# Attention kernel on one core: rotary sine terms by exchanging even and odd partitions in SBUF

## What is computed

```python
xn = _layernorm(x, ln1_g, ln1_b)
q = _l2norm((xn @ Wq).reshape(Bx, Tx, H, Dh))
k = _l2norm((xn @ Wk).reshape(Bx, Tx, H, Dh))
q = _rope(q, times)
k = _rope(k, times)
...
# _rope
xr = x.reshape(*x.shape[:-1], half, 2)
x1, x2 = (xr[..., 0], xr[..., 1])
r1 = x1 * cos - x2 * sin
r2 = x1 * sin + x2 * cos
```

## Time and profile before

| what | value |
|---|---|
| runs | 2165.68, 2159.67, 2165.37 us, median 2165.37 |
| profiled execution | span 2164.4 us; its own time is not given apart from the three above, the span is 1.0 us below their median |
| granted TensorE clock, mean | 0.931 of 2.4 GHz; 1.00 in the stretches of attention from 50 to 650 us |
| 300 to 350 us (attention), busy of 50 us | TensorE 48.06, VectorE 40.44, ScalarE 43.75, GpSimd 12.59 |
| a full step, from one start of L807 to the next | 41.83 us (324.63 to 366.46) |
| 300 to 350 us, DMA | 9% of the 16 engines, 28 GB/s |

### The profile page before, as it was taken

One profiled execution on the slowest core, in us unless ns is written; L12 is line 12 of the kernel. 1 busy time (PEld: TensorE's weight loads), 2 busy tenths in 40 slices (PEclk: granted clock), 3 DMA queues, 4 the chain that ended last, 5 costly groups with the idle time before them and its releaser, 6 DMA issues. The chain is left out here.

```text
span 2164.4 us, 37241 instructions
## 1 busy us (share of the span) xinstructions
PE 1849.2 (85%) x12576; PEld 954.5 (44%) x12600; DVE 1703.8 (79%) x3547; ACT 1474.7 (68%) x2917; POOL 1165.1 (54%) x720
## 2 busy tenths in 40 slices
PE   6999999999998459957889889898898988659996
PEld 2566666656665259952222222222222222124453
DVE  7778868877863437854899999999999998976776
ACT  5888888888885138845656666666666666437775
POOL 2122232242221027871789999999999998840001
PEclk9999999999999669977899999999999998879998
DMA  4100010011001012221100111001111100023333
GB/s 169 36 26 26 28 49 26 26 36 41 21 25 33 20 50 77 88 72 42 30 25 27 34 35 34 27 30 30 31 35 35 35 31 30 21 67 90 97 84 78
DMA packets 103708, 97.35 MB, mean 45 GB/s; under 512 B 9137, under 2 KB 86113, under 8 KB 103137
## 3 DMA queue, kind: packets, MB, share of 16 engines
q1 hardware_dynamic: 95584, 75.34, 12.4%
q0 software_dynamic: 6784, 18.10, 2.5%
q10 hardware_dynamic: 1152, 1.54, 0.2%
HBM read 45.87 MB, written 28.10 MB: 34 GB/s over the span
## 5 line engine op out<-in xcount | busy, mean ns | idle before, releaser
L1935 POOL TENSOR_TENSOR hc<-h,c_rep 128x1024 f32<-128x1024 f32 x256 | 627.8, 2463 | 137.9 <-DVE h L1899 136.7
L1899 DVE TENSOR_TENSOR_SCAN h<-decay,bank 128x1024 f32<-128x1024 f32 x241 | 551.0, 2286 | 22.5 <-issue 0.9
L1757 ACT ACTIVATE decay<-bank,neg_a_r 128x510 f32<-128x510 f32 x512 | 322.6, 683 | 257.5 <-PE bank L1634 257.1
L1618 PE MATMUL bank<-u_in,sel_rows 32*128 32x512 f32 x964 | 287.9, 675 | 95.7 <-DVE h L1899 95.6
L1634 PE MATMUL bank<-delta,sel_rows 32*128 32x512 f32 x1024 | 338.8, 677 | 0.9 <-ACT decay L1757 0.9
L1886 DVE TENSOR_TENSOR bank<-bank,b_rep 128x1024 f32<-128x1024 f32 x241 | 291.2, 1208 | 34.8 <-PE bank L1618 33.0
L992 POOL DMA_INDIRECT rows_in_dram<-row,idx x64 | 63.3, 989 | 318.3 <-DVE row L965 303.7
L574 ACT ACTIVATE es<-bank 128x384 f32<-128x384 f32 x512 | 208.9, 499 | 22.1 <-PE bank L373 21.8
L1618 PEld LDWEIGHTS bank<-u_in,sel_rows 32*128 32x128 f32 x964 | 76.0, 191 | 276.7 <-DVE h L1899 199.7
L1649 PE MATMUL bank<-hc,y_sel 128*32 128x512 f32 x1024 | 149.6, 660 | 0.8 <-POOL hc L1935 0.8
L1656 PE MATMUL bank<-xpad,w_conv 128*128 128x512 f32 x256 | 133.0, 634 | 3.2 <-ACT xc L1819 1.6
(11 more groups left out here) (341 smaller groups left out, 4170.0 us busy)
## 6 DMA issues: line engine op xcount, KB each, us to landing
r_tw<-r_o_t SPq DMA_DIRECT2D x96, 128.0 KB, 2.3
xvs<-xv SPq DMA_DIRECT2D x16, 512.0 KB, 2.9
u_wide<-u_rep_dram SPq DMA_DIRECT2D x30, 256.0 KB, 3.5
xs<-rows_in_dram SPq DMA_DIRECT2D x72, 68.0 KB, 1.8
front<-in_x_dram SPq DMA_DIRECT2D x16, 256.0 KB, 2.9
w<-in_w_dram SPq DMA_DIRECT2D x2, 2048.0 KB
xlb_dram<-front SPq DMA_DIRECT2D x16, 256.0 KB, 2.3
xlb_m<-xlb_dram SPq DMA_DIRECT2D x16, 256.0 KB
```

The costliest lines, as they stand in the source:

```text
L1618: last = pe.matmul(BD[n % 2][:, i * STEP:(i + 1) * STEP], sel[at:at + 32, r, :], u_in[p if n < NS else q][at:at + 32, hf, :], start=True, ...
L1757: act.activation(decay[n % 4][:, i, :, 1:], seq(DL[i])[:, :, 1:], ACT.Exp, scale=c["neg_a_r"][:, hf, g:g + 1]).then_inc(s["n_da"], 1)
L1899: dve.tensor_tensor_scan(flat(h[n % RING]), decay[n % 4].rearrange("p i b t -> p (i b t)"), flat(drive_0) if by_pool else BD[n % 2], 0.0, ...
L1935: pool.tensor_tensor(hc[n % RING][:, :, :], h[n % RING][:, :, :], c_rep[p if n < NS else q][:, :].unsqueeze(1).to_broadcast([P, 2, STEP]), ...
```

## The change

The projections `w_qs` and `w_ks` are left out. Instead the query in PSUM is multiplied by `sin` at once (`rot_b`), and two transfers copy its odd partitions to the even ones of a new tile `rot_s` and its even partitions to the odd ones (`swap`, on SyncE's queue). The sum becomes `rot - rot_s`: the sign in the table now belongs to the neighbour. The key goes the same way, through the same two tiles. The weight tile `w_a` loses the 256 columns, and its load is split into three DMAs on ScalarE's queue; two small tables of the end of the part (`of`, `before`) move into `log`.

```diff
+        def swap(sp, sem):
+
+            for to in range(2):
+                sp.dma_start(rot_s[to:P:2, :], rot_b[1 - to:P:2, :]).then_inc(sem, 16)
...
             if front:
 
+                sp.wait_ge(s["f_rb"], one_on)
+                swap(sp, s["f_qsw"])
+                sp.wait_ge(s["f_kb"], one_on)
+                sp.wait_ge(s["f_rq"], one_on)
+                swap(sp, s["f_ksw"])
                 sp.wait_ge(s["f_xlb"], one_on)
                 sp.dma_start(rows(d["xlb"], here), xl[:, :, :]).then_inc(s["xlb_stored"], 16)
...
-            if front:
-                pe.wait_ge(s["f_pe"], k + 1)
-                project(FB, c["w_qs"], s["f_qs"])
...
-                pe.wait_ge(s["f_ra"], k + 1)
+                pe.wait_ge(s["f_rb"], k + 1)
                 pe.matmul(FA[:, :], c["ones_blk"], square[:, :], start=True, stop=True).then_inc(s["f_ssq"], 1)
-                pe.wait_ge(s["f_rb"], k + 1)
+                pe.wait_ge(s["f_pe"], k + 1)
                 project(FB, c["w_k"], s["f_k"])
...
-            if front:
-                pe.wait_ge(s["f_mq"], k + 1)
-                project(FA, c["w_ks"], s["f_ks"])
...
-                pe.wait_ge(s["f_ka"], k + 1)
+                pe.wait_ge(s["f_kb"], k + 1)
                 pe.wait_ge(s["f_sk"], k + 1)
...
                 dve.tensor_tensor(seq(rot), seq(FA), cos, ALU.mult).then_inc(s["f_ra"], 1)
+                since(dve, s["f_ksw"], 32 * k)
+                dve.tensor_tensor(seq(rot_b), seq(FA), sin, ALU.mult).then_inc(s["f_rb"], 1)
             if tail:
                 dve.wait_ge(s["m_st2"], k - 2)
                 bn_aggr(mv_m, stats_m, s["m_mv2"])
-            if front:
-                dve.wait_ge(s["f_qs"], k + 1)
-                since(dve, s["f_rk"], k)
-                dve.tensor_tensor(seq(rot_b), seq(FB), sin, ALU.mult).then_inc(s["f_rb"], 1)
...
-            if front:
-                dve.wait_ge(s["f_ra"], k + 1)
-                dve.wait_ge(s["f_rb"], k + 1)
-                dve.tensor_tensor(rot[:, :], rot[:, :], rot_b[:, :], ALU.add).then_inc(s["f_rq"], 1)
...
+                dve.wait_ge(s["f_ra"], k + 1)
+                dve.wait_ge(s["f_qsw"], 32 * k + 32)
+                dve.tensor_tensor(rot[:, :], rot[:, :], rot_s[:, :], ALU.subtract).then_inc(s["f_rq"], 1)
...
-                dve.wait_ge(s["f_ks"], k + 1)
-                dve.wait_ge(s["f_rq"], k + 1)
-                dve.tensor_tensor(seq(rot_b), seq(FA), sin, ALU.mult).then_inc(s["f_kb"], 1)
...
                 dve.tensor_tensor(seq(rot_k), seq(FB), cos, ALU.mult).then_inc(s["f_ka"], 1)
+                dve.wait_ge(s["f_qsw"], 32 * k + 32)
+                dve.tensor_tensor(seq(rot_b), seq(FB), sin, ALU.mult).then_inc(s["f_kb"], 1)
...
-                dve.wait_ge(s["f_kb"], k + 1)
-                dve.tensor_tensor(rot_k[:, :], rot_k[:, :], rot_b[:, :], ALU.add).then_inc(s["f_rk"], 1)
+                dve.wait_ge(s["f_ksw"], 32 * k + 32)
+                dve.tensor_tensor(rot_k[:, :], rot_k[:, :], rot_s[:, :], ALU.subtract).then_inc(s["f_rk"], 1)
...
-            act.dma_start(c["w_a"][:, :], dram["w_a"]).then_inc(s["p_small"], 16)
+            act.dma_start(c["w_a"][:, 0:4 * D], dram["w_a"][:, 0:4 * D]).then_inc(s["p_small"], 16)
+            act.dma_start(c["w_a"][:, 4 * D:5 * D], dram["w_a"][:, 5 * D:6 * D]).then_inc(s["p_small"], 16)
+            act.dma_start(c["w_a"][:, 5 * D:], dram["w_a"][:, 7 * D:]).then_inc(s["p_small"], 16)
```

24 lines of the change are left out of this document (13 added, 11 removed).

## The result

The changed kernel takes **2198.8 us** (median of 4 runs, 2192.2 to 2205.7) against 2162.5 for the kernel before (4 runs): ratio **1.017, 95% interval 1.015 to 1.019**, 36 us slower. The forecast was 2176. The direction was right, the size was not: +10 forecast, +36 measured, outside the range.

What follows compares the result with a forecast made beforehand. A step was taken as a loop of VectorE's half, then TensorE's, the projections lying beside VectorE's. 13 x (0.66 + 0.13) = 10.3 us added to 2165.4 gave 2176 us; own range 2171 to 2181, 8 in 10 2163 to 2184.

Steps and rivals of the forecast that it cites:

- Step 1: TensorE: two projections removed, 31 us of its time, worth 0 in 13 full steps, -2 us in steps 1 and 2.
- Steps 2, 3 and 5: VectorE in the attention stage: `h_tok` 0.60 us later; L832 0.11 later, moved sum adds 0.60; clip waits 0.11 to 0.13.
- step 4: VectorE and GpSimd at `xl`: `mag` begins when the moved sum ends, `xl` ends 0.66 us later, bounds 0.47 and 0.92.
- Step 6: Swap transfers: 3.4 us in all, hidden behind 5.6 and 5.4 us of cover; likeliest cost 0, bounds 0 and 0.3 a step.
- Step 7: Prologue, steps 0 to 2: uncovered swaps +2 us, gain of 2 us, together 0, give or take 2.
- The rivals: VectorE keeps the port: 2166 us, chance 0.2; TensorE is the bound: 2134 us, 0.08; swap late: 2194 us, 0.06.

Runs made afterwards that it cites:

- r_before: The kernel before itself, run again beside the others for its profile; 2166.7 us (one run).
- r_after: The changed kernel itself, run again in the second group; ratio 1.017 to the kernel before.
- e4_one: The changed kernel with one unused projection (`w_k` into `FA`) put back directly ahead of TensorE's idle time; ratio 1.007 to the kernel before.
- e3_again: The changed kernel with the first sine product behind `bn_aggr` again and its sum between scan and clip; ratio 1.002 to the kernel before.
- e2_order: The kernel before with VectorE's new order alone, all projections kept and no transfer; ratio 1.005 to the kernel before.
- e14_inter: `e3_again` with `rot_k`'s product and the second `rot_b` product between `xl` pieces, ScalarE's square of `FB` ahead of its `xt`; ratio 0.9986 to the kernel before.
- e5_noproj: The kernel before without its two sine projections and without transfers, the exchange of neighbours left out; ratio 1.009 to the kernel before.
- e12_behind: The changed kernel with both projections put back unused, directly behind the `xl` transposes; ratio 1.016 to the kernel before.
- e15_q_only: The changed kernel with one unused projection (`w_q` into `FB`) put back 8 us ahead of the idle time; ratio 1.017 to the kernel before.

## Why the prediction was wrong

The account of the 39 us between the spans of `r_before` and `r_after`, from the starts of steps 3 and 16 in each:

| part | forecast | measured | from |
|---|---|---|---|
| steps 0 to 2 | 0, give or take 2 | +6.7 | step 3 at 122.63 against 115.95 |
| 13 full steps, order of VectorE | +10.3 | +9.4 | `e4_one` 553.07 against 543.67 |
| 13 full steps, granted clock | 0 | +26.3 | 579.33 against 553.07 |
| the rest of the program | 0 | -3.5 | the rest to 38.8 |

**Step 1 failed, and with it the size.** It said that TensorE's idle time before the `xl` transposes "should grow from 1.05 to about 3 us" and was "worth 0 there". The part on the path was right: the projections lie ahead of a wait for VectorE, and leaving them out gives nothing (`e3_again`, 41.84 us a step). But idle time on TensorE is not free when it grows: the granted clock falls behind it, and the matmuls up to the affinities take up to 1.7 times as long (0.64 to 1.08), on a path that has no slack. `e4_one` against `r_after` gives 1.4 us for a step with one low stretch (43.95 against 42.54) and 3.1 for one with two. That cost was 26.3 of the 38.8 us, and the sum had no term for it. The clock row of the kernel before said 1.00 for every full step, and I took that as a property of the stage and not of the 1.05 us. The size of the gap itself was off too, 2.23 against 3.6: of the 1.92 us that TensorE was spared, 0.61 reached the gap, since it now also waits for ScalarE earlier in the step.

**Steps 2, 3 and 5 held, step 4 in its size.** `h_tok` comes 0.59 later (forecast 0.60), L832 0.10 (0.11), `xl` 0.57 (0.66, bounds 0.47 and 0.92), and the clip waits for the scan's end (361.25 in the timeline). But `mag` was not held until the moved sum ended, as step 4 had it: it starts at 356.76, 0.47 us later in the step than before, which is ScalarE's delay alone, and 0.18 us before the sum ends (356.26 + 0.68); the other 0.10 is in `mag` and `log`, 0.05 us longer each. And the small `row` did take the slip of the first `xl` piece, for which the upper bound of 0.92 stood, without that price. GpSimd's times are rough, so a tenth or two should not be built on. In sum 0.72 us a step by `e4_one` and 0.81 by `e2_order`, where 0.79 stood.

**Step 6 held in full steps**: no wait for a transfer, 2.1 us to land where 2.3 had been taken. `e3_again` and `e14_inter` confirm it.

**Step 7 failed by 6.7 us.** I counted a gain of 2 us from VectorE's waits for `w_ks` and forgot that the norm's matmul must now wait for both query products, since they share a bank; the diff has it (`f_ra` became `f_rb` at L481). In full steps this is hidden; in the first ones it is not. Leaving out the projections, with this wait, makes 4.5 us alone (`e5_noproj`, 120.44), and the transfers add 0.2 to that (`e3_again`, 120.68). The new order makes 0.6 alone (`e2_order`) and 2.0 on top of the two (122.63 - 120.68). These come from different chips, and how much of them is the clock (three low stretches from 32 to 67 us in `r_after`, where the kernel before has one) was not taken apart.

**The rivals.** None of the three was right, and none was about the clock. The one rule of the Trainium skill that spoke against the change, that of the section on TensorE's clock named above, under which the forecast's own 3.6 us of idle time would have been too long, was not weighed; I took the one on VectorE's port instead. The 3.5 us at the end of the table were not followed up; the part behind step 15 differs by up to 10 us between the profiles of the later groups.

## What to carry to other kernels

Before costing removed TensorE work at nothing, look at the granted clock of that stretch and at how long TensorE then idles: here 1.4 us of idle time kept the clock, 2.2 us lost it in every step of the changed kernel, and one projection whose result nobody reads, placed directly ahead of the idle time, made the kernel 24 us faster (2200.4 to 2176.8). A wait of VectorE for GpSimd could be filled with products that have one input in a PSUM bank (0.6 us a step in `e14_inter`). And the first steps of a pipeline need their own account, since a wait that is hidden in a full step can stand open there.

## What was not expected of the hardware

- Two kernels with the same 2.23 us of idle time, `e12_behind` and `e15_q_only`, lose the clock in 3 and in 13 of 13 steps; in the first, two projections stand directly behind the idle time, in the second, one stands 8 us ahead of it.
- In the changed kernel the fall comes back near the same place in each step, 0.1 to 1.5 us behind the start of the `xl` transposes in steps 4 to 15, and in every fourth step (6, 10, 14) the clock stays low twice as long, 6.8 us instead of 3.4, which makes 45.6 us instead of 43.95. Both profiles of it show this; that of `e15_q_only` has it in steps 7, 11 and 15. Why every fourth is open.
- A transfer of 64 partitions from odd to even ones, 2 KB each, lands in 2.1 us (median), no slower than those of the earlier trace rows (2.3), which exchange the upper and the lower 64 partitions.
